# Key tokens in tiles of 128, z copies by way of DRAM, a new opening, one product moved from VectorE, and new program orders

## The chip, the cores and the metric

The kernel runs on one core of a Trainium2 chip. The metric is the device time of one execution in microseconds (us); a kernel is judged by the median of several runs. The engines are TensorE (PE; its weight loads are listed as PEld), VectorE (DVE), ScalarE (ACT), GpSimd (POOL) and SyncE (SP), which here only starts transfers (DMAs). Each engine works through its own program in order and waits on semaphores.

## The reference

The input x holds 32 images of 56 x 56 pixels with 32 channels, in f32. For each image, in short:

```python
x = x + conv3x3(sign(batchnorm(groupnorm(x))), sign(W) * scale)
t = tokens(x)                                   # 3136 tokens of 32 channels
n = layernorm(t)
q, k, v = elu(n@wq + b) + 1, elu(n@wk + b) + 1, n@wv + b         # 16 heads of 32
kv_cos, kv_sin = sum_s (k*cos)^T v, sum_s (k*sin)^T v            # linear attention
o = (q*cos)@kv_cos + (q*sin)@kv_sin
t = t + dense(o / (q*cos . sum k*cos + q*sin . sum k*sin + 1e-5))
n2 = layernorm(t)
w = the two largest of softmax(n2 @ router), scaled to sum 1
t = t + sum over those two of w_e * (n2 @ expert_e + b_e)        # 8 experts
```

The statistics of the batch norm go over all 32 images, so all of x is read once before any image can begin.

## The kernel before

**Tiling.** An image's 3136 tokens lie in 7 tiles. A tile holds 112 patches of 2 x 2 pixels, so there are 28 slots (7 tiles by 4 pixel positions g) of 112 tokens. In "patch layout" a matrix has 128 rows (4 positions by 32 channels) and 784 patches.

**Steps.** The work on an image is cut into named steps, and each engine does its share of a step. XT loads the image and turns it; CV is the convolution (SP copies the thresholded image `nat` to `shifted` first); XC centers it, SM1 and PN1 make the first layernorm `xn`. ZT turns `xn` back and splits it into a high and a low f16 half, `zhl`. SP then copies `zhl` into `z1`, 16 DMAs (lines 464 to 471), so that each of the four g has its high and low rows on 128 partitions. ZU does the same for the second layernorm, into `z2`. K computes keys: two matmuls of 512 columns (line 551), an exponential on ACT (688), a max/min on DVE into `kbuf` (975), two buffers. KX multiplies the keys with `xcs`, the tokens times cos and sin, which POOL makes in CS (797); its two matmuls are in f32 and write the two halves of one bank (560). KT and G turn the sum into the matrices for the queries. Q computes queries like K (576, 693, 981). DN, SU, RC, RL and RH make the reciprocal of the denominator. R and RP spread it over the heads with a matmul (602) and multiply the queries: channel half 0 of each of the 7 tiles on DVE, straight from the bank (R, line 996), half 1 by an ACT copy into `spread_r` (725) and a POOL product (802) (RP). NM and T2 form the attention output; S2, SM2 and PN2 the second layernorm; LG and RT the router; F the experts (DVE 1058, POOL 841 to 847); OUT the store.

**Order.** The order of the steps on each engine is written out by hand in the table `ORDER`: each step has a time in units of which 14 make one iteration, and each iteration of the walk runs the steps of up to seven images, shifted against each other. Most matmul results go to a ring of three pairs of banks (K, Q, R, RP, F, ...); a step takes a pair when the step three places before it in PE's order has been read. SP, too, is in order: it waits for what a transfer needs, starts it, and goes on to the next.

**Opening.** SP loads x in eight parts of four images into two buffers `stage`; PE turns them, DVE takes their statistics. Then come the weights and the tables. PE begins with the first image when ACT has folded `wv` and `wd` into `p2`, DVE has the thresholds and all tables are there.

Of the kernel before, what the change touches and what calls it, by code (L numbers as in the profile page):

```python
# [6 lines left out]
F32 = mybir.dt.float32  # L7
# [15 lines left out]
TOKENS = HW * HW  # L23
DH = HEADS * C
# [3 lines left out]
HALF = (4, 3)  # L28
COL = [(0, 4 * PT), (4 * PT, 7 * PT)]
# [9 lines left out]
def consts():  # L39
# [31 lines left out]
    tabk = cs.transpose(3, 0, 1, 2).reshape(PT, 2 * SLOTS)  # L71
# [21 lines left out]
class Img:  # L93
# [10 lines left out]
    def par(self):  # L104
# [29 lines left out]
    },  # L134
    "vector": {
# [16 lines left out]
    },  # L152
    "scalar": {
# [17 lines left out]
    },  # L171
    "gpsimd": {
        "RP": [20.36, 21.80, 23.22, 26.00, 26.75, 27.35, 28.06],
        "F": [42.89, 44.35, 45.46, 46.69, 47.39, 51.02, 52.51],
        "T2": [26.80, 29.79, 32.86, 34.18],
        "RL": [19.34, 24.68],
        "CS": [-1.95, 6.49],
        "PN2": [35.08],
        "PN1": [-4.03],
        "OUT": [54.08],  # L180
        "RF": [40.46, 40.76],
        "GT": [41.80],
    },
    "sync": {
        "OUT": [42.36],
        "ZT": [-9.43],
        "CV": [-23.34],
        "XT": [-35.15],
        "ZU": [24.07],
# [51 lines left out]
def build(nc, x, gamma, beta, conv_taps, conv_rows, wq, wk, wv, wd, wd_b, we, eyec, eyem, mean4, pair, dsum, sel,  # L241
          p2c, tabdc, tabnc, tabkc, firstc, validc, out):
    ctx = ExitStack()
    with ctx:
# [16 lines left out]
        tabk = sb("tabk", [PT, 2, SLOTS])  # L261
# [28 lines left out]
        xcs = sb("xcs", [PT, SLOTS, 2, C])  # L290
# [3 lines left out]
        kbuf = sb("kbuf", [PT, 2, 1024])  # L294
# [19 lines left out]
        stage = [qflat[0:PT, k * 3584:(k + 1) * 3584].rearrange("p (b f) -> p b f", b=4) for k in range(2)]  # L314
# [28 lines left out]
        weights_in = sem("weights_in")  # L343
        tables_in = sem("tables_in")
# [3 lines left out]
        stage_in = [sem(f"stage_in{k}") for k in range(2)]  # L348
# [23 lines left out]
        zlow_made = [sem(f"zlow_made{k}") for k in (1, 2)]  # L372
        z_in = [sem(f"z_in{k}") for k in (1, 2)]
# [36 lines left out]
        READ = {"K": (k_made, 14), "R": (qr_made, 7), "RP": (r_copied, 7), "Q": (q_made, 14), "G": (g_made, 2),  # L410
# [8 lines left out]
        def _(sp):  # L419
            sp.dma_start(eye_center[:, :], eyec).then_inc(eye_in, 16)  # L420
            x4 = x.rearrange("(q b) h w c -> q b (h w c)", b=4).rearrange("q b (p f) -> q p b f", p=PT)
            for k in range(2):
                sp.dma_start(stage[k], x4[k]).then_inc(stage_in[k], 16)
# [60 lines left out]
        def _(pe):  # L484
# [3 lines left out]
            for q in range(8):  # L488
                pe.wait_ge(stage_in[q % 2], 16 * (q // 2) + 16)
                for b in range(4):  # L490
                    if 4 * q + b >= 4:
                        pe.wait_ge(stage_read, 4 * q + b - 3)
                    for j in range(TILES):
                        dst = ps[:, 2 * b + (j >= 4), (j % 4) * PT:(j % 4 + 1) * PT]
                        mm = pe.transpose(dst, stage[q % 2][:, b, j * 128:(j + 1) * 128], eye[0:PT, 0:PT])
                    mm.then_inc(stage_turned, 1)
# [7 lines left out]
            pe.wait_ge(weights_in, 16 * 11)  # L504
            pe.wait_ge(dve_pre, 4)
            for h in range(HEADS):
                mm = pe.matmul(ps[:, 2, C * h:C * h + C], wvr[:, 128 * h:128 * h + 128], wd_s[:, C * h:C * h + C], start=True, stop=True)
            mm.then_inc(pe_pre, 1)

            def step(kind, m, n, rd):  # L510
# [34 lines left out]
                elif kind == "K":  # L545
                    pe.wait_ge(z_in[0], m.at(256, 256))
                    if n == 0:
                        pe.wait_ge(weights_made, 1)
                    for k in range(2):
                        s = 2 * n + k  # L550
                        mm = pe.matmul(o[0:PT, k, :], z1[:, m.par, s % G, s // G, :], wk16[:, :], start=True, stop=True)  # L551
                    mm.then_inc(ring_full, 1)
                elif kind == "KX":
                    pe.wait_ge(k_made, m.at(14, n + 1))
                    if n in (0, 7):
                        pe.wait_ge(xcs_made, m.at(2, n // 7 + 1))
                    if n == 0:
# [555 lines left out]
```

## Time and profile before

| | |
|---|---|
| median of 3 runs | 2426.46 us (2424.11 to 2431.5) |
| the profiled execution's own time | 2426.23 us |
| its span, from the first to the last instruction | 2424.4 us |
| busy, share of the span | PE 93%, DVE 85%, ACT 66%, POOL 76% |
| 16 DMA engines, share of the span | 21.3% |
| matmuls | 15908 |

Busy shares are means over an opening, a long middle part in which images follow each other, and an end. The rows that the prediction uses stand in a section of their own below.

### The profile page before, as it was taken

Reading aid. Unit: us, or ns where it says so; the run is one execution under the profiler, and the core shown is the slowest. Engines: PE = TensorE matmul, PEld = TensorE weight load, DVE = VectorE, ACT = ScalarE, POOL = GpSimd, SP = SyncE. Lnnn points to the kernel's source line nnn. Section 1 sums busy time; section 2 is a strip of 40 time slices with the busy share of each in tenths; the row PEclk is TensorE's granted clock in tenths of the full one; section 3 lists DMA queues with packets and bytes.
Section 4 is the critical chain, followed back from the end, with each engine's and each line's share of the span. In section 5 each row is a group of like instructions: output and inputs, shape, how many; then the busy total and the mean of one; then the engine's idle time right before and its main releaser. Section 6 shows DMA issues by size and latency. Waiting matters only on the chain.

```text
span 2424.4 us, 45391 instructions
## 1 busy us (share of the span) xinstructions
PE 2252.8 (93%) x15908; PEld 1126.0 (46%) x15908; DVE 2064.4 (85%) x2725; ACT 1589.9 (66%) x2789; POOL 1841.0 (76%) x1553
## 2 busy tenths in 40 slices
PE   4369999999999999999999999999999999999971
PEld 4324444444544444444544444454544444454441
DVE  5357899999999999999999999999999999998852
ACT  0157777777777777777777777777777777777620
POOL 0414588888888888888888888888888888888775
PEclk8589999999999999999999999999999999999985
DMA  7421112222221112222221212222211212211001
GB/s 209 112 39 22 32 29 44 35 42 45 45 44 34 36 34 43 34 44 44 45 42 36 34 37 40 35 45 45 45 39 37 37 36 40 36 38 35 21 21 27
DMA packets 284863, 105.31 MB, mean 43 GB/s; under 512 B 246032, under 2 KB 279680, under 8 KB 284512
## 3 DMA queue, kind: packets, MB, share of 16 engines
q1 hardware_dynamic: 284640, 102.41, 21.3%
q8 instruction: 131, 2.15, 0.4%
q14 instruction: 92, 0.75, 0.1%
HBM read 31.19 MB, written 12.85 MB: 18 GB/s over the span
## 4 chain that ended last, share of the span: by engine, by line
PE 67%; DVE 15%; ACT 6%; issue 5%; POOL 3%; DMA 2%; SPq 1%; POOLq 0%; DVEq 0%; ACTq 0%
PE ps L560 15%; PE ps L611 12%; PE ps L551 7%; PE ps L602 6%; PE ps L576 5%; PE ps L585 5%; DVE qbuf L981 4%; DVE prod L1058 4%; ACT ebuf L693 3%; DVE kbuf L975 3%; PE ps L542 2%; PE ps L535 2%; PE ps L630 2%; DVE den L993 2%; PE ps L530 2%
## 5 line engine op out<-in xcount | busy, mean ns | idle before, releaser
L975 DVE SCALAR_TENSOR_TENSOR kbuf<-ps,ebuf 112x1024 f32<-112x1024 f32 x448 | 546.2, 1219 | 114.3 <-ACT ebuf L688 111.8
L693 ACT ACTIVATE ebuf<-ps,small 128x896 f32<-128x896 f32 x448 | 450.3, 1005 | 195.0 <-PE ps L576 113.1
L688 ACT ACTIVATE ebuf<-ps,small 112x1024 f32<-112x1024 f32 x448 | 498.3, 1112 | 107.4 <-PE ps L551 87.8
L981 DVE SCALAR_TENSOR_TENSOR qbuf<-ps,ebuf 128x896 f32<-128x896 f32 x448 | 486.5, 1086 | 43.2 <-ACT ebuf L693 38.7
L802 POOL TENSOR_TENSOR qbuf<-spread_r,qbuf 128x896 f32<-128x896 f32 x224 | 469.0, 2094 | 21.4 <-ACT spread_r L725 21.4
L560 PE MATMUL ps<-kbuf,xcs 112*64 112x512 f32 x1792 | 474.9, 613 | 4.1 <-DVE kbuf L975 4.1
L785 POOL TENSOR_TENSOR rstd<-varr,power 112x28 f32<-112x28 f32 x64 | 307.2, 4800 | 137.7 <-DVE varr L960 137.5
L611 PE MATMUL ps<-qbuf,gmat 128*64 128x224 f32 x3584 | 390.1, 360 | 3.0 <-POOL qbuf L802 2.2
L611 PEld LDWEIGHTS ps<-qbuf,gmat 128*64 128x64 f32 x3584 | 243.7, 138 | 165.0 <-issue 77.8
L1058 DVE TENSOR_TENSOR prod<-ps,gate 112x1024 f32<-112x1024 f32 x224 | 271.2, 1212 | 29.6 <-POOL ffn L847 10.1
L551 PE MATMUL ps<-wk,z 128*112 128x512 f16 x896 | 280.1, 395 | 15.7 <-issue 12.6
L841 POOL TENSOR_TENSOR prod<-prod 112x512 f32<-112x512 f32 x224 | 285.5, 1275 | 1.5 <-DVE prod L1058 1.4
L725 ACT ACTIVATE spread_r<-ps 128x896 f32<-128x896 f32 x224 | 204.6, 913 | 82.2 <-PE ps L602 53.8
L576 PE MATMUL ps<-z,wq 128*128 128x448 f16 x896 | 245.5, 356 | 6.2 <-DVE qbuf L981 3.3
L602 PE MATMUL ps<-rs,sel 128*128 128x448 f16 x896 | 240.8, 357 | 10.5 <-ACT rs L719 4.3
L996 DVE TENSOR_TENSOR qbuf<-ps,qbuf 128x896 f32<-128x896 f32 x224 | 237.3, 1083 | 7.2 <-PE ps L602 4.6
L585 PE MATMUL ps<-qbuf,dmat 128*32 128x448 f32 x1792 | 231.9, 549 | 0.2
L551 PEld LDWEIGHTS ps<-wk,z 128*112 128x112 f16 x896 | 93.6, 129 | 206.7 <-DVE qbuf L981 74.0
L844 POOL TENSOR_TENSOR prod<-prod 112x256 f32<-112x256 f32 x224 | 163.4, 730 | 17.6
L560 PEld LDWEIGHTS ps<-kbuf,xcs 112*64 112x64 f32 x1792 | 101.7, 136 | 146.5 <-issue 116.1
L636 PE MATMUL ps<-we,z 128*112 128x256 f16 x896 | 145.0, 287 | 11.2 <-DVE prod L1058 10.4
L636 PEld LDWEIGHTS ps<-we,z 128*112 128x112 f16 x896 | 97.1, 133 | 83.3 <-issue 24.1
(131 smaller groups left out, 3052.6 us busy)
## 6 DMA issues: line engine op xcount, KB each, us to landing
z<-zhl SPq DMA_DIRECT2D x1024, 49.0 KB, 1.9
qbuf<-in_x SPq DMA_DIRECT2D x8, 1568.0 KB, 8.9
xt<-in_x SPq DMA_DIRECT2D x256, 49.0 KB
out<-ffn SPq DMA_DIRECT2D x256, 49.0 KB
shifted<-nat SPq DMA_DIRECT2D x128, 52.6 KB, 5.0
qbuf<-in_sel SPq DMA_DIRECT2D x1, 1024.0 KB, 13.2
tabn<-in_tabnc SPq DMA_DIRECT2D x1, 784.0 KB, 12.5
p<-in_p2c SPq DMA_DIRECT2D x1, 528.0 KB, 9.6
```

What stands on the lines that cost most here:

```text
L551: mm = pe.matmul(o[0:PT, k, :], z1[:, m.par, s % G, s // G, :], wk16[:, :], start=True, stop=True)
L560: mm = pe.matmul(kt_bank[64 * k:64 * k + 64, :], xcs[:, 2 * n + k, :, :].rearrange("p a c -> p (a c)"), kbuf[:, n % 2, DH * k:DH * k + DH] ...
L576: mm = pe.matmul(o[:, k, 0:G * PT].rearrange("p (g t) -> p g t", g=G), wq16[:, 128 * (k0 + k):128 * (k0 + k) + 128], z1[:, m.par, :, j, :] ...
L585: mm = pe.matmul(o[32 * j:32 * j + 32, 0:HW4], dmat[:, m.par, c, :, :].rearrange("p a h -> p (a h)"), qbuf[:, c, 4 * h + j, :], start=(c = ...
L602: mm = pe.matmul(o[:, k, 0:HW4], sel16[:, 128 * a:128 * a + 128], rs[:, j // 4, :], start=True, stop=True)
L611: mm = pe.matmul(o[64 * v:64 * v + 64, 0:2 * PT].rearrange("p (a t) -> p a t", a=2), gmat[:, m.par, c, :, :].rearrange("p a o -> p (a o)") ...
L688: act.activation(ebuf[0:PT, 0, :].rearrange("p (a b) -> p a b", a=2), o[0:PT, :, :], ACT.Exp, bias=minus_one[0:PT, :]).then_inc(kexp_made, 1)
L693: act.activation(ebuf[:, 1, 0:2 * G * PT].rearrange("p (a b) -> p a b", a=2), o[:, :, 0:G * PT], ACT.Exp, bias=minus_one).then_inc(qexp_ma ...
L802: nc.gpsimd.tensor_tensor(qbuf[:, 2:4, n, :], spread_r[:, :, :], qbuf[:, 2:4, n, :], ALU.mult)\
L975: v.scalar_tensor_tensor(kbuf[:, n % 2, :].rearrange("p (a b) -> p a b", a=2), o[0:PT, :, :], 1.0, ebuf[0:PT, 0, :].rearrange("p (a b) -> ...
L981: v.scalar_tensor_tensor(qbuf[:, k0:k0 + 2, j, :], o[:, :, 0:G * PT], 1.0, ebuf[:, 1, 0:2 * G * PT].rearrange("p (a b) -> p a b", a=2), AL ...
L1058: v.tensor_tensor(prod[:, n % 2, :, :].rearrange("p s (e c) -> p (s e) c", c=C), o[0:PT, :, :].rearrange("p k (s c) -> p (k s) c", c=C), g ...
```

## The change

- **Keys.** Keys are computed for 24 tiles of 128 tokens and one of 64 instead of 28 of 112: `KT` = 25 matmuls in `KS` = 13 steps, for K and for KX. The tokens for KX must lie in the same tiles: SP writes `xn` to a DRAM tensor `xd` (four DMAs, step CS0 of SP) and reads it back as `xkt` (two DMAs, CS1), and POOL makes `xcs` from `xkt`.
- **z.** The 16 copies become one store of `zhl` to DRAM (`zd`), a wait of SP for it, and four loads.
- **The queries' product.** For tile 1 both halves are done the RP way; R has 6 steps and RP 8.
- **Opening.** x goes through four buffers of two images; the first image's own load stands ahead of the weights; the weights are in two groups with a semaphore each; `wv` times `wd` goes to bank 7, and ACT's fold into `p2` and the waits for the tables move into the steps that first need them.
- **Program orders.** All five lists of `ORDER` are new.

```diff
+KT = -(-TOKENS // 128)
+KREST = TOKENS - 128 * (KT - 1)
+KS = (KT + 1) // 2
+KH = 6
+BOTH = (1,)
+R_TILES = [j for j in range(TILES) if j not in BOTH]
+RP_UNITS = [(j, h) for j in range(TILES) for h in ((1, 0) if j in BOTH else (1,))]
...
-            for k in range(2):
-                sp.dma_start(stage[k], x4[k]).then_inc(stage_in[k], 16)
+            for q in range(4):
+                sp.dma_start(stage[q], x2[q]).then_inc(stage_in[q], 16)
...
-            for q in range(2, 8):
-                sp.wait_ge(stage_turned, 4 * q - 4)
-                sp.dma_start(stage[q % 2], x4[q]).then_inc(stage_in[q % 2], 16)
+            for q in range(4, B // 2):
+                sp.wait_ge(stage_turned, 2 * q - 6)
+                sp.dma_start(stage[q % 4], x2[q]).then_inc(stage_in[q % 4], 16)
...
+            load(Img(None, 0))
...
                     sp.wait_ge(zlow_made[ln], m.at(2, 2))
+                    wait(sp, z_in[ln], m.at(64))
+                    sp.dma_start(zd[ln], zhl[ln][:, :, :]).then_inc(z_out[ln], 16)
+                    sp.wait_ge(z_out[ln], m.at(16, 16))
+                    src = zd[ln].rearrange("(g c) h f -> h c g f", g=G)
                     for r in range(4):
-                        for g in range(G):
-                            dst = z2[32 * r:32 * r + 32, g] if ln else z1[32 * r:32 * r + 32, m.par, g]
-                            sp.dma_start(dst.rearrange("p j t -> p (j t)"),
-                                         zhl[ln][32 * g:32 * g + 32, r % 2, :]).then_inc(z_in[ln], 16)
+                        dst = z2[32 * r:32 * r + 32] if ln else z1[32 * r:32 * r + 32, m.par]
+                        sp.dma_start(dst.rearrange("p g j t -> p g (j t)"), src[r % 2]).then_inc(z_in[ln], 16)
+                if kind == "CS" and n == 0:
+                    sp.wait_ge(xn_made[0], m.at(1, 1))
+                    wait(sp, xkt_in, m.at(32))
+                    for g in range(G):
+                        dst = xd[PATCHES * g:PATCHES * g + PATCHES].rearrange("(j t) c -> t j c", t=PT)
+                        src = xn[0][:, :, :].rearrange("p (j g) c -> p g j c", g=G)[:, g]
+                        sp.dma_start(dst, src).then_inc(xkt_out, 16)
+                if kind == "CS" and n == 1:
+                    sp.wait_ge(xkt_out, m.at(64, 64))
+                    wait(sp, xcs_made, m.at(2))
+                    sp.dma_start(xkt[:, 0:KT - 1, :], xd[0:128 * (KT - 1)].rearrange("(i p) c -> p i c", p=128)).then_inc(xkt_in, 16)
+                    sp.dma_start(xkt[0:KREST, KT - 1, :], xd[128 * (KT - 1):TOKENS]).then_inc(xkt_in, 16)
...
-                    for k in range(2):
-                        s = 2 * n + k
-                        mm = pe.matmul(o[0:PT, k, :], z1[:, m.par, s % G, s // G, :], wk16[:, :], start=True, stop=True)
+                    flat = z1[:, m.par, :, :, :].rearrange("p g j t -> p (g j t)")
+                    for k in range(2 if n < KS - 1 else 1):
+                        a, w = 128 * (2 * n + k), 128 if 2 * n + k < KT - 1 else KREST
+                        mm = pe.matmul(o[0:w, k, :], flat[:, a:a + w], wk16[:, :], start=True, stop=True)
...
-                    for k in range(2):
-                        mm = pe.matmul(kt_bank[64 * k:64 * k + 64, :],
-                                       xcs[:, 2 * n + k, :, :].rearrange("p a c -> p (a c)"),
-                                       kbuf[:, n % 2, DH * k:DH * k + DH], start=(n == 0), stop=(n == 13))
+                    for k in range(2 if n < KS - 1 else 1):
+                        i = 2 * n + k
+                        w = 128 if i < KT - 1 else KREST
+                        mm = pe.matmul(kt_bank[64 * k:64 * k + 64, :], xcs[0:w, i, :, :].rearrange("p a c -> p (a c)"),
+                                       kbuf[0:w, m.at(KS, n) % 2, DH * k:DH * k + DH], start=(n == 0), stop=(i >= KT - 2))
...
-            pe.wait_ge(act_pre, 1)
             pe.wait_ge(dve_pre, 6)
-            pe.wait_ge(tables_in, 16 * 9)
...
-                    nc.gpsimd.tensor_tensor(qbuf[:, 2:4, n, :], spread_r[:, :, :], qbuf[:, 2:4, n, :], ALU.mult)\
+                    j, half = RP_UNITS[n]
+                    q = qbuf[:, 2 * half:2 * half + 2, j, :]
+                    pool.wait_ge(r_copied, m.at(NP, n + 1))
+                    nc.gpsimd.tensor_tensor(q, spread_r[:, :, :], q, ALU.mult)\
```

In the new order one iteration of SP is: XT, ZU, CS0, CV, ZT, CS1, OUT (before: OUT, ZT, CV, XT, ZU). A stretch of PE's new order, from ZU to LG, is: ZU1, K10, XT0, KX8, RP3, Q1, XT1, KX9, K11, NM1, RP4, R1, KX10, R2, ZT0, Q2, NM2, R3, RP5, LG. From ZT to the next image's first KX it is: ZT1, T20, R4, Q4, Q5, NM3, RP7, Q6, KX12, NM4, G0, G1, NM5, R5, Q7, T21, F0, Q8, T22, F1, Q9, DN0, DN1, F2, Q10, DN2, K0, DN3, K1, Q11, SU0, K2, NM6, KX0; then F3, K3, KX1, RP0, KX2, T23, R0, F4, K4. (T20 to T23 are the four steps T2.)

## Rows read from the trace of the kernel before

**Rows 1.** Stretch, its us, busy (count) PE, PEld, DVE, ACT, POOL; clock, DMA, GB/s.
```profile
1000.00:1200.00 200.00, 199.35 (x1431) 98.54 (x1427) 183.62 (x240) 146.19 (x258) 166.40 (x139) 1.00 0.20 39
```

**Rows 2.** The chain that ended last, whole run: start us, us, what.
```profile
282.76 1.87 PE ps L560 x8
...
2194.53 1.87 PE ps L560 x8
```

**Rows 3.** The same chain, within one image's period.
```profile
1016.81 0.57 PE ps L551 x2
...
1028.10 0.86 PE ps L560 x4
...
1029.88 0.43 PE ps L551 x2
1030.31 1.01 PE ps L560 x4
...
1036.83 1.67 PE ps L611 x16
1038.49 0.53 PE ps L542 x4
...
1042.39 0.40 PE ps L602 x2
...
1044.45 0.48 PE ps L602 x2
```

**Rows 4.** Groups of instructions: shapes, count; busy us, mean ns; idle before.
```profile
L975 DVE SCALAR_TENSOR_TENSOR kbuf<-ps,ebuf 112x1024 f32<-112x1024 f32 x448 | 546.2, 1219 | 114.3 <-ACT ebuf L688 111.8 <-PE ps L560 0.3
...
L560 PE MATMUL ps<-kbuf,xcs 112*64 112x512 f32 x1792 | 474.9, 613 | 4.1 <-DVE kbuf L975 4.1
L802 POOL TENSOR_TENSOR qbuf<-spread_r,qbuf 128x896 f32<-128x896 f32 x224 | 469.0, 2094 | 21.4 <-ACT spread_r L725 21.4
...
L996 DVE TENSOR_TENSOR qbuf<-ps,qbuf 128x896 f32<-128x896 f32 x224 | 237.3, 1083 | 7.2 <-PE ps L602 4.6
...
L797 POOL TENSOR_TENSOR xcs<-xn,tabk 112x448 f32<-112x448 f32 x128 | 117.8, 942 | 0.2
```

**Rows 5.** Timeline from a ZU to the LG that needs its z: start, us.
```profile
1026.25 0.89 PE L542 MATMUL ps<-eye_center,xn 112*128 112x112 f32 x7
...
1028.54 10.29 SPq L470 DMA_DIRECT2D z<-zhl  x16
...
1040.82 1.36 PE L630 MATMUL ps<-we,z 128*112 128x8 f16 x24
```

**Rows 6.** DMA issues: count, KB each, median us from issue to landing.
```profile
z<-zhl SPq DMA_DIRECT2D x1024, 49.0 KB, 1.9
qbuf<-in_x SPq DMA_DIRECT2D x8, 1568.0 KB, 8.9
...
shifted<-nat SPq DMA_DIRECT2D x128, 52.6 KB, 5.0
```

**Rows 7.** The chain in the opening, 0 to 70 us.
```profile
27.41 8.67 DMA qbuf<-in_x
...
55.38 8.61 DMA qbuf<-in_x
...
64.04 4.20 PE ps L495 x21
```

**Rows 8.** Busy time by engine in a stretch of the opening.
```profile
30.00:40.00 10.00, 4.21 (x25) 4.00 (x24) 4.97 (x11) 0.00 (x0) 0.00 (x0) 0.73 1.03 273
```

**Rows 9.** Timeline of the opening, all engines.
```profile
82.91 1.28 ACT L654 ACT_TABLE_LOAD   x1 [82.91 <-PE ps L507]
...
84.56 0.15 DVE L927 COPY small<-small 128x1 f32<-128x1 f32 x1
...
86.64 1.01 PE L521 MATMUL ps<-eye_center,xt 112*128 112x112 f32 x4 [3.82 <-ACT p L654]
...
130.65 1.93 PE L551 MATMUL ps<-wk,z 128*112 128x512 f16 x4 [12.61 <-issue]
```

More of the change, by code:

```diff
@@ L152 @@
+        "SM1": [-11.08],
+        "ZU": [30.95, 31.39],
+        "XT": [-24.26, -24.17],
+        "RC": [11.46, 18.02],
+        "R": [12.96, 18.69, 18.77, 19.28, 20.57, 23.13],
+        "ZT": [-9.06, -7.96],
+        "LG": [33.34],
+        "RT": [34.58, 35.36, 35.96, 36.51, 36.71, 37.05],
     },
     "scalar": {
[17 rows of a table removed]
+        "ZU": [28.02, 28.71],
+        "K": [-4.42, -3.99, -2.45, -1.94, -1.52, -1.14, -0.84, -0.49, -0.21, 0.23, 0.78, 1.80, 4.55],
+        "SU": [9.97, 14.55],
+        "XT": [-27.01, -26.78],
@@ new lines @@
+        "RP": [12.12, 12.54, 13.65, 15.08, 16.64, 17.30, 18.72, 20.70],
+        "Q": [-0.36, 1.78, 3.10, 4.69, 5.31, 6.03, 6.94, 7.41, 8.09, 8.51, 9.01, 10.04, 12.89, 13.27],
+        "RC": [10.14, 16.27],
+        "RH": [11.87, 16.66],
+        "ZT": [-11.25, -8.84],
+        "LG": [32.59],
+        "T2": [19.24, 21.94, 22.17, 26.18],
+        "KT": [6.83],
+        "RT": [35.03],
+        "G": [7.18, 7.40],
+        "S2": [24.99, 25.88, 26.49, 27.04],
+        "TB": [12.37],
+        "XC": [-14.01],
@@ L171 @@
     },
     "gpsimd": {
[L173 to L182, printed above, removed]
+        "RP": [10.18, 13.67, 14.95, 16.87, 18.30, 19.00, 19.14, 20.76],
+        "F": [35.33, 35.65, 37.08, 37.38, 38.24, 43.15, 46.85],
@@ L183 @@
+        "PN1": [-12.27],
+        "RL": [9.31, 16.89],
+        "OUT": [47.05],
+        "RF": [33.10, 33.36],
+        "T2": [19.80, 20.90, 23.37, 24.21],
+        "GT": [34.66],
+        "CS": [-5.29, -4.67],
+        "PN2": [27.73],
     },
     "sync": {
[L185 to L189, printed above, removed]
+        "XT": [-41.69],
+        "ZU": [14.70],
+        "CS": [-24.14, -16.17],
+        "CV": [-36.65],
+        "ZT": [-19.15],
@@ L190 @@
+        "OUT": [39.95],
     },
@@ L313, in build @@
         qflat = qbuf[:, :, :, :].rearrange("p a b c -> p (a b c)")
-        stage = [qflat[0:PT, k * 3584:(k + 1) * 3584].rearrange("p (b f) -> p b f", b=4) for k in range(2)]
+        stage = [qflat[0:PT, k * 1792:(k + 1) * 1792].rearrange("p (b f) -> p b f", b=2) for k in range(4)]
         at, views = 2 * 3584, {}
@@ L343, in build @@
         weights_in = sem("weights_in")
+        folds_in = sem("folds_in")
         tables_in = sem("tables_in")
@@ L347, in build @@
         eye_in = sem("eye_in")
-        stage_in = [sem(f"stage_in{k}") for k in range(2)]
+        stage_in = [sem(f"stage_in{k}") for k in range(4)]
         stage_turned = sem("stage_turned")
@@ L372, in build @@
         zlow_made = [sem(f"zlow_made{k}") for k in (1, 2)]
+        zd = [nc.dram_tensor(f"zd{k}", [128, 2, PATCHES], F16).ap() for k in (1, 2)]
+        z_out = [sem(f"z_out{k}") for k in (1, 2)]
+        xd = nc.dram_tensor("xd", [TOKENS, C], F32).ap()
+        xkt_out = sem("xkt_out")
+        xkt_in = sem("xkt_in")
         z_in = [sem(f"z_in{k}") for k in (1, 2)]
@@ L487, in _ @@
             pe.wait_ge(eye_in, 16)
[L488 to L496, printed above, removed]
+            for img in range(B):
+                q, b = img // 2, img % 4
+                pe.wait_ge(stage_in[q % 4], 16 * (q // 4) + 16)
+                if img >= 4:
+                    pe.wait_ge(stage_read, img - 3)
+                for j in range(TILES):
+                    dst = ps[:, 2 * b + (j >= 4), (j % 4) * PT:(j % 4 + 1) * PT]
+                    mm = pe.transpose(dst, stage[q % 4][:, img % 2, j * 128:(j + 1) * 128], eye[0:PT, 0:PT])
+                mm.then_inc(stage_turned, 1)
             pe.wait_ge(consts_in, 16 * 5)
@@ L605, in step @@
                 elif kind == "NM":
-                    pe.wait_ge(qr_made, m.at(7, n + 1))
-                    pe.wait_ge(qp_made, m.at(7, n + 1))
+                    wait(pe, qr_made, m.at(NR, len([j for j in R_TILES if j <= n])))
+                    pe.wait_ge(qp_made, m.at(NP, len([j for j, _ in RP_UNITS if j <= n])))
                     for c in range(CH):
@@ L647, in _ @@
         def _(act):
-            act.wait_ge(tables_in, 16 * 9)
-            act.wait_ge(pe_pre, 3)
-            for v in range(2):
-                for cs in range(2):
-                    q = slice(64 * v + 32 * cs, 64 * v + 32 * cs + 32)
-                    dst = p2[q, :, cs, :, 0:C]
-                    last = act.activation(dst, ps[q, 2, :].rearrange("p (a h o) -> p a h o", a=CH, h=HPC), ACT.Copy,
-                                          scale=SHIFT)
-            last.then_inc(act_pre, 1)
             act.wait_ge(dve_pre, 6)
@@ L680, in step @@
                     ln = kind == "ZU"
+                    if m.c == 0 and n == 0 and kind == "ZT":
+                        act.wait_ge(tables_in, 16 * 9)
+                        act.wait_ge(pe_pre, 3)
+                        for v in range(2):
+                            for cs in range(2):
+                                q = slice(64 * v + 32 * cs, 64 * v + 32 * cs + 32)
+                                last = act.activation(p2[q, :, cs, :, 0:C],
+                                                      ps[q, 7, :].rearrange("p (a h o) -> p a h o", a=CH, h=HPC), ACT.Copy,
+                                                      scale=SHIFT)
+                        last.then_inc(act_pre, 1)
                     act.wait_ge(ring_full, no + 1)
-                    wait(act, z_in[ln], m.at(256))
+                    wait(act, z_out[ln], m.at(16))
                     a, b = COL[n]
@@ L713, in step @@
                     act.wait_ge(recip_made, m.at(2, n + 1))
-                    wait(act, qr_made, m.at(7, -3 if n == 0 else 0))
+                    wait(act, qr_made, m.at(NR, -len([j for j in R_TILES if j >= 4]) if n == 0 else 0))
                     act.activation(r_high[:, :], den[:, 0:HALFW], ACT.Copy).then_inc(rhigh_made, 1)
@@ L788, in step @@
                     wait(pool, high_made[ln], m.at(2))
+                    if not ln:
+                        wait(pool, xkt_out, m.at(64))
                     nc.gpsimd.tensor_tensor(xn[ln][:, :, 0:C - 1], xc[ln][:, :, 0:C - 1],
@@ L867, in _ @@
             v.memset(nat[:, :, :], 1.0)
+            v.memset(xkt[:, KT - 1:KT, :], 0.0)
             v.memset(dmat[:, :, :, :, :], 0.0)
@@ L984, in step @@
                 elif kind == "DN" and n % 4 == 3:
+                    if m.c == 0 and n == 3:
+                        dve.wait_ge(tables_in, 16 * 9)
                     h = n // 4
```

105 lines of the change are left out of this document (61 added, 44 removed), and 67 rows, old and new, of the table ORDER.

## The prediction, made before the change was run

> **What bounds the kernel now.** I first read a stretch in the middle of the run by engine [rows 1]. The reader is to see that TensorE (PE) is busy 199.35 of 200 us at the full granted clock, VectorE (DVE) 183.62, GpSimd (POOL) 166.40 and ScalarE (ACT) 146.19, with DMA at 0.20. Next I read the chain of the whole run [rows 2]: the same double KX step comes back at 282.76 and at 2194.53 us, 28 images later, so an image costs 68.28 us and 31 images after the first cost 2117 of the 2424.4 us. Then I read one period of that chain [rows 3]. Its pieces are PE steps laid end to end; a K step (two matmuls) takes 0.43 or 0.57 us, a KX step 0.86 or 1.01. So PE's list of steps is the period, and an edit is worth what it takes off that list, as long as no other engine or transfer then holds PE up. The opening (first K of the first image at 130.65 us, [rows 9]) and the end, where one image runs alone, are chains of waits of their own.
>
> **Fewer K and KX steps.** Before, an image has 28 slots of 112 tokens: 14 K steps and 14 KX steps. After, it has 25 tiles of 128 (the last of 64): 13 steps each, the last of one matmul. From [rows 3]:
> - KX: one step less, 0.86 to 1.01 us; I take 0.95. The four records of a step last 0.61 us each on average [rows 4] but a step is over in 0.86, so its two matmuls, which write different halves of the bank, run beside each other. The single matmul of the last step therefore saves nothing more.
> - K: one step less, 0.43 to 0.57; I take 0.50. The last step has one matmul instead of two: half of 0.43, 0.21.
> Together 1.66 us an image (1.50 to 1.79). DVE loses two K passes of 1.22 us and gets one half as wide (about 0.69, by the width), 1.75 us less; ACT loses in the same proportion.
>
> **One product moved.** Tile 1's first half leaves DVE (1.08 us) and goes to ACT (one more copy) and POOL (2.09) [rows 4]. PE's matmuls for it stay. DVE now needs 62.7 - 1.75 - 1.08 = 59.9 us an image (183.62/200 of 68.28, less these), 90% of a 66.6 us period where it had 92%. POOL needs 56.8 + 2.09, and its CS passes shrink from 3.77 to 25/28 of that, so 58.5 us, 88% of the period where it had 83%. Both still end inside the period, so I cost the move at nothing; it is PE's list that hides it. If that cover went, it would cost POOL's 2.09 less DVE's 1.08, about 1 us an image.
>
> **New program orders.** The order of PE's steps changes everywhere, and a step's cost depends on its neighbour by some 0.15 us [rows 3]; kinds follow each other about as often as before, so I take no difference. DVE is locally the denser engine between F0 and the next image's K4, where five F and five K passes (K's takes 1.22 us, [rows 4]) stand close together. Three ring slots lie between PE and DVE, so I bound what PE waits there by nothing and one such pass, 1.22 us, and take 0.15, since DVE's share falls. Per image: -1.66 + 0.15, about -1.5; over 31 images **-46.5 us** (-55 to -9).
>
> **z by way of DRAM.** The 16 copies of z (16 issues in 10.29 us, then 1.9 us to land [rows 5, 6]) become one store to DRAM, a wait on SP for it, and four loads. No row of before shows a store to DRAM that is waited for. From below I take the 1.9 us of the small copy; from above I add the size: a load of 1568 KB lands in 8.9 us [rows 6], 0.0046 us a KB more, so 392 KB would take 3.5 us, and the last loads, 784 KB in all, 1.9 to 3.4 us after the last issue. From the last ZU matmul to the first copy is 1.4 us before (1027.14 to 1028.54, [rows 5]). After: 1.4 + 0.64 + 1.9 (3.5) + 4 x 0.64 + 1.9 (3.4) + 0.1 = 8.5 to 11.6 us; I take 10.5, nearer the upper end because that one counts the bytes. What is behind this is LG, which needs z of the second layernorm. In the new PE order there lie between ZU1 and LG two K, three KX, six R or RP, two Q, two NM, two XT and one ZT step. With Q priced like K, R at 0.40 to 0.48 and the last three at no more than 0.53 each, that is 1.0 + 2.9 + 2.6 + 0.9 + 3.3 + 1.3 = 12.0 us [rows 3]. So LG just does not wait; before, it was the same race (12.3 us from first issue to LG, [rows 5]). The Trainium skill (DMA: Bandwidth & Descriptors, Anatomy of one DMA) speaks against this edit: it puts about 2.0 us of fixed cost on each DMA, most of it the receipt of the write and heaviest where the target is HBM, and here it is paid twice in a row; no row here shows such a receipt. By its fit (2.0 us plus the bytes at 436 GB/s, for another way of issuing) I estimate the path at 10.1 us, and the sum would be the same.
>
> SP stands still while it waits for that store. Behind it in SP's order are CS1 (the reload of the keys' tokens), OUT and the next XT load; the latter two are due most of a period later. The first layernorm's z is followed by K0, and the keys' tokens go out (four DMAs of 784 pieces of 128 bytes) and come back (3072 pieces): 1.4 + 0.64 + 3.5 + 2.6 + two issues 1.3 + 5.0 (what a shift of 928 pieces of 58 bytes takes, [rows 6]) + two CS passes 1.9 = 16.3 us from ZT1 to KX0. Between those stand four NM, one KX, eight Q, three R or RP and three K steps, 6.7 + 1.0 + 3.6 + 1.3 + 1.5 = 14.1 us, and thirteen steps of other kinds not counted in it. So it fits, at no cost.
>
> **The opening.** Before, PE waits three times for x, 8.67 us the first time and 8.61 the last [rows 7], since a part's load starts only when its buffer was read. The 8 loads of 1568 KB are 12.8 MB; at the 273 GB/s of the stretch from 30 to 40 us [rows 8] they need 47 us, and PE's 224 transposes, at 4.20 us for 21, 44.8 us. With four buffers of half the size both overlap: the transposes end at best near 51 us instead of 68.2 (-17), at worst one wait goes (-8); I take -13. PE no longer waits for ACT's work on p2 (start 86.64 against 84.71 when DVE is done, [rows 9]: -1.9), but the table load (1.28) moves behind the first threshold: -0.6. On the other side, SP now issues four stores of xn and the second image's four shifts before z of the first image: eight issues of 0.64 us, partly under the ZT steps, so some 3 us later, and z and then xkt queue behind their small pieces; KX0 needs xkt, which it did not before. I put that at +4.5 (0 to +10). Together **-9 us** (-19 to +2). **The end**: one ZU path of 12.3 us becomes about 10.5, **-2** (0 to -4).
>
> **The sum**, on the profiled execution: 2424.4 - 46.5 - 9 - 2 = 2366.9 us of span, and 1.8 us lie around the span (its time is 2426.23): 2368.7. The median of the three runs, 2426.46, is 0.2 above that execution, so 2369.
>
> **Rivals.**
> - *DVE or POOL becomes the bound* in part of the period (DVE between F0 and K4, or POOL, whose 58.5 us also hold waits for the routing and for spread_r). For it: both are at 90% and 88%, and they run lists in fixed order. Against it: DVE's load falls. A period of 67.4 to 68.0 us gives 2392 to 2416.
> - *LG waits for z*, the rival on the other side. The price is 31 us for each us by which the path outlasts 12.0 us. It takes back the whole gain (57.5 us) when it is late by 1.9 us, that is with a path of 13.9 us; at 14.5 us the kernel takes 2446. For it: a stored and waited-for DRAM write is unknown here, and the margin is 0 to 3 us. Against it: even the size-counting end is 11.6 us, and the queue is not loaded (DMA 0.20). The Trainium skill's rule on the write's receipt (same page, same section) is this mechanism.
> - *The change is hidden*: the period shrinks by half a us and the opening by nothing, 2419 to 2434. PE's list would have to be no bound, against [rows 1].
> - *Better ends on all terms*: 2424.4 - 55 - 19 - 4 + 1.8 = 2348 and a little below.
>
> **How the numbers follow.** Forecast as summed, 2348 to 2392: 0.55. DVE or POOL: 0.19. LG late: 0.12. Hidden: 0.06. Better: 0.08. A measurement of this kernel tells about 0.3% (7 us) from no change. Faster is 0.55 + 0.19 + 0.08 = 0.82, same 0.06, slower 0.12. The predicted time is 2369 us. The range 2342 to 2414 takes in the forecast, nearly all of the second case and most of the better one, about 8 in 10.
>
> **What would show it.** In the profile after: the same KX step recurring every 66.5 to 67 us; 13 KX and 13 K steps an image; PE still above 99% busy in the middle; DVE near 90%, POOL near 88%; no recurring wait of LG for z or of POOL's CS for xkt; the last bn_stats near 55 us; the first K near 122 to 127 us. I am wrong if PE is well below 99% in the middle, with LG or a K step waiting for a DMA, or with the ring waiting for DVE, or if the period is right and the opening is not shorter.

## The result and the profile after

The changed kernel takes 2417.58 us (median of 11 runs, 2402.14 to 2421.86) where the kernel before takes 2427.9 in the same comparison (2424.11 to 2433.57): a ratio of 0.9947, 95% interval 0.993 to 0.9964. The forecast was 2369 us, in a range of 2342 to 2414, so the prediction was wrong: faster, but by 10 us and not by 57. The profiled execution took 2408.88 us, with a span of 2407.1; it is the second shortest of the 11, so the median execution is some 9 us longer than the one that the rows below show.

In the middle of the run, by engine (columns as in [rows 1]):

```profile
1000.00:1200.00 200.00, 195.94 (x1432) 95.56 (x1430) 179.01 (x233) 145.84 (x260) 171.96 (x142) 1.00 0.35 65
...
1800.00:2000.00 200.00, 194.20 (x1418) 94.26 (x1414) 179.35 (x231) 143.56 (x259) 174.76 (x147) 1.00 0.35 61
```

Against [rows 1] TensorE has lost its 99%: 3.4 to 5.2 us more idle time in 200, and VectorE and ScalarE are no busier. Only GpSimd and the DMA engines work more. No engine is full, so something that is no engine's work sets the pace.

How long an image takes is read from an instruction that occurs once in it. I take POOL's step OUT (line 878, in which `ffn` and `t` are added), here in POOL's timeline for the first image and for the 28th (after that one the images run out and the gaps shrink):

```profile
352.61 2.09 POOL L878 TENSOR_TENSOR ffn<-ffn,t 112x896 f32<-112x896 f32 x1
...
2200.50 2.08 POOL L878 TENSOR_TENSOR ffn<-ffn,t 112x896 f32<-112x896 f32 x1
```

27 gaps in 1847.89 us are 68.44 us each. The same instruction in the kernel before:

```profile
360.72 2.09 POOL L835 TENSOR_TENSOR ffn<-ffn,t 112x896 f32<-112x896 f32 x1
...
2204.91 2.09 POOL L835 TENSOR_TENSOR ffn<-ffn,t 112x896 f32<-112x896 f32 x1
```

These are gaps of 68.30, as the recurring step of [rows 2] says. **The steady part gained nothing**; it lost 3.7 us. The 17.3 us between the two spans come from the ends, which gained 21.0: the first OUT is 8.1 us earlier, and from the 28th OUT to the last instruction it takes 206.6 us, not 219.5.

What sets the 68.44 shows in the chain that ended last, here from one image's OUT to the next image's first F on POOL:

```profile
1589.35 1.99 POOL ffn L878
...
1591.36 0.52 DVE zhl L1014
...
1591.90 2.35 DMA zd<-zhl
...
1594.27 0.31 SPq L493
...
1596.10 0.38 SPq L504
...
1596.52 3.40 SPq L505
...
1604.83 1.71 DMA out<-ffn
...
1606.67 1.28 POOL prod L884
```

SP holds the output for 8.6 us after it is ready. POOL's OUT is over at 1591.4, but SP has just begun on z: the store of `zhl` (2.35 us until it has landed), four loads (1.73 in all), two loads of key tokens, of which the second and small one (64 tokens) takes 3.40 us to issue. Only at 1599.96 does it reach the eight stores of the output (5.28 us), and the last of them lands at 1606.54. POOL waits for that landing, because F of the next image writes the one buffer `ffn` (line 883, a wait on `out_stored`). POOL's timeline around it, the bracket being the idle time and its releaser:

```profile
1604.28 0.63 POOL L850 TENSOR_TENSOR xc<-t,mean 112x256 f32<-112x256 f32 x1
1606.67 1.27 POOL L884 TENSOR_TENSOR prod<-prod 112x512 f32<-112x512 f32 x1 [1.76 <-DMA out<-ffn]
```

The page's groups give the whole run's idle time in that place (last columns), and the sizes of the other edited steps:

```profile
L884 POOL TENSOR_TENSOR prod<-prod 112x512 f32<-112x512 f32 x224 | 285.6, 1275 | 79.9 <-DMA out<-ffn 55.7
...
L597 PE MATMUL ps<-kbuf,xcs 128*64 128x512 f32 (+1 forms) x1600 | 449.4, 619 | 3.2 <-POOL xcs L838 1.8
...
L1043 DVE TENSOR_TENSOR qbuf<-ps,qbuf 128x896 f32<-128x896 f32 x192 | 208.6, 1086 | 11.6 <-PE ps L641 9.4
```

The reader is to see 55.7 us of waiting for `out<-ffn`, most of what the image period is above the 66.2 us that turn out below (27 times 2.2, or 60). The edits themselves came out as planned: 1600 KX records in place of 1792 at the same length as in [rows 4], 192 passes of R on VectorE in place of 224.

DMA issues of the new paths (count, KB each, median us from issue to landing):

```profile
z<-zd SPq DMA_DIRECT2D x256, 196.0 KB, 3.7
zd<-zhl SPq DMA_DIRECT2D x64, 392.0 KB, 2.4
...
xkt<-xd SPq DMA_DIRECT2D x32, 384.0 KB, 6.3
```

The opening, in PE's and POOL's timelines: last transposes of x, the first image's XT, its first K, its first CS.

```profile
60.69 2.88 PE L529 MATMUL ps<-eye_center,qbuf 112*128 112x112 f32 x14 [0.50 <-DMA qbuf<-in_x]
77.33 1.01 PE L555 MATMUL ps<-eye_center,xt 112*128 112x112 f32 x4
...
124.65 2.72 PE L586 MATMUL ps<-wk,z 128*128 128x512 f16 x6 [14.58 <-issue]
...
127.38 3.31 POOL L838 TENSOR_TENSOR xcs<-xkt,tabk 128x384 f32<-128x384 f32 x4 [18.93 <-DMA xkt<-xd]
```

In PE's timeline of the kernel before, the last transposes of x are these:

```profile
64.04 5.18 PE L495 MATMUL ps<-eye_center,qbuf 112*128 112x112 f32 x28 [5.73 <-DMA qbuf<-in_x]
```

Transposes end at 63.57 (69.22 before; the chain of [rows 7] leaves TensorE after 21 of these 28, at 68.24), XT starts at 77.33 and K at 124.65 (86.64 and 130.65, [rows 9]).

### The profile page after: what moved, and what is told of

Read it like the earlier page. It is cut to its first block, busy times and chain, and to the rows that moved or that the text cites. A ratio compares the mean times of both kernels' runs of the same rounds, so it can differ in the third digit from the quotient of the medians.

```text
span 2407.1 us, 44360 instructions
## 1 busy us (share of the span) xinstructions
PE 2201.8 (91%) x15620; PEld 1085.5 (45%) x15620; DVE 2001.0 (83%) x2662; ACT 1566.6 (65%) x2789; POOL 1898.4 (79%) x1585
## 4 chain that ended last, share of the span: by engine, by line
POOL 38%; PE 25%; SPq 10%; issue 8%; DVE 7%; DMA 7%; ACT 4%; POOLq 0%; DVEq 0%; ACTq 0%
POOL qbuf L845 11%; POOL rstd L824 8%; POOL prod L884 6%; PE ps L597 5%; PE ps L650 4%; SPq L511 4%; SPq L505 4%; POOL prod L887 4%; POOL xn L830 3%; DMA zd<-zhl 3%; PE ps L614 2%; PE ps L641 2%; PE ps L586 2%; PE ps L623 2%; DVE kbuf L1019 2%
## 5 line engine op out<-in xcount | busy, mean ns | idle before, releaser
L845 POOL TENSOR_TENSOR qbuf<-spread_r,qbuf 128x896 f32<-128x896 f32 x256 | 536.1, 2094 | 31.9 <-ACT spread_r L764 28.6
L1019 DVE SCALAR_TENSOR_TENSOR kbuf<-ps,ebuf 128x1024 f32<-128x1024 f32 (+1 forms) x416 | 488.3, 1174 | 83.1 <-ACT ebuf L727 72.2
L727 ACT ACTIVATE ebuf<-ps,small 128x1024 f32<-128x1024 f32 (+1 forms) x416 | 449.3, 1080 | 138.5 <-PE ps L586 83.5
L597 PE MATMUL ps<-kbuf,xcs 128*64 128x512 f32 (+1 forms) x1600 | 449.4, 619 | 3.2 <-POOL xcs L838 1.8
L884 POOL TENSOR_TENSOR prod<-prod 112x512 f32<-112x512 f32 x224 | 285.6, 1275 | 79.9 <-DMA out<-ffn 55.7
L764 ACT ACTIVATE spread_r<-ps 128x896 f32<-128x896 f32 x256 | 234.3, 915 | 114.3 <-PE ps L641 67.5
L586 PE MATMUL ps<-wk,z 128*128 128x512 f16 (+1 forms) x800 | 249.4, 391 | 63.3 <-DVE prod L1105 33.3
L1043 DVE TENSOR_TENSOR qbuf<-ps,qbuf 128x896 f32<-128x896 f32 x192 | 208.6, 1086 | 11.6 <-PE ps L641 9.4
L641 PEld LDWEIGHTS ps<-rs,sel 128*128 128x128 f16 x896 | 61.9, 100 | 209.2 <-issue 87.9
L586 PEld LDWEIGHTS ps<-wk,z 128*128 128x128 f16 (+1 forms) x800 | 61.0, 98 | 200.9 <-DVE prod L1105 66.9
L597 PEld LDWEIGHTS ps<-kbuf,xcs 128*64 128x64 f32 (+1 forms) x1600 | 85.3, 135 | 142.3 <-issue 126.4
## 6 DMA issues: line engine op xcount, KB each, us to landing
qbuf<-in_x SPq DMA_DIRECT2D x16, 784.0 KB, 10.3
```

The lines of the kernel that those rows point to most:

```text
L586: mm = pe.matmul(o[0:w, k, :], flat[:, a:a + w], wk16[:, :], start=True, stop=True)
L597: mm = pe.matmul(kt_bank[64 * k:64 * k + 64, :], xcs[0:w, i, :, :].rearrange("p a c -> p (a c)"), kbuf[0:w, m.at(KS, n) % 2, DH * k:DH * k ...
L641: mm = pe.matmul(o[:, k, 0:HW4], sel16[:, 128 * a:128 * a + 128], rs[:, j // 4, :], start=True, stop=True)
L727: act.activation(ebuf[0:w, 0, 0:DH * c].rearrange("p (a b) -> p a b", a=c), o[0:w, 0:c, :], ACT.Exp, bias=minus_one[0:w, :]).then_inc(kexp ...
L845: nc.gpsimd.tensor_tensor(q, spread_r[:, :, :], q, ALU.mult)\
L884: nc.gpsimd.tensor_tensor(p[:, :, 0:4 * C], p[:, :, 0:4 * C], p[:, :, 4 * C:], ALU.add)\
```

## The experiments

Three theories went into the first four. **A**: a closed loop, in which SP holds the store of the output behind z and the key tokens, POOL's F waits for it, and the delay comes back through the period to the same place. **B**: POOL has too much work since the product moved. **C**: TensorE or VectorE waits for z or key tokens from DRAM.

**1. The store of the output ahead of z on SP.**

```diff
-        "OUT": [39.95],
+        "OUT": [36.80],
```

> Edit: in SP's program order the store of an image (OUT) stands ahead of ZT's store and loads and of CS1, instead of last; nothing else differs from the changed kernel. Theory A (a closed loop: POOL's F0 waits until the previous image's output is stored, the store is issued by SP only after ZT and CS1, ZT waits for ACT, ACT for POOL's products): the loop is cut, the period falls from 67.9 us to between 66.4 and 67.2 us (it may be held a little by the key tokens, which now come about 5 us later), 2370 to 2395 us, ratio to the kernel before 0.976 to 0.986. Theory B (POOL simply has too much work, 175 of 200 us): period stays 67.9, ratio 0.995. Theory C (PE or DVE waits for z or the key tokens from DRAM): later ZT makes it slower, ratio above 1.0.

Measured: 2344.99 us, ratio 0.9665 (0.9651 to 0.968). POOL's OUT of the first and 28th image, and the middle by engine:

```profile
351.57 2.08 POOL L878 TENSOR_TENSOR ffn<-ffn,t 112x896 f32<-112x896 f32 x1
...
2139.11 2.10 POOL L878 TENSOR_TENSOR ffn<-ffn,t 112x896 f32<-112x896 f32 x1
```

```profile
1400.00:1600.00 200.00, 198.40 (x1455) 97.23 (x1456) 184.58 (x239) 147.60 (x263) 177.68 (x149) 1.00 0.34 67
```

27 gaps of 66.21 us. SP's timeline shows why:

```profile
1611.31 3.57 SPq L511 DMA_DIRECT2D out<-ffn  x8
1614.98 0.35 SPq L488 DMA_DIRECT2D zd<-zhl  x1
```

POOL's OUT ends at 1611.28 and the store is issued in the same moment; F0 starts at 1624.76, 13.5 us after OUT. In the changed kernel POOL is at F0 equally 13.5 us after OUT (1606.67 less 1.76, against 1591.4), but the store lands after 15.1. With the store first, POOL no longer waits for it (its row has 21.6 of its 21.7 us of idle time from VectorE), z leaves 3.2 us after its data is ready, and in the middle of the run nothing waits for it. TensorE is busy again for 198.4 of 200 us, and the chain's share of PE goes from 25% to 80%. A stands, but the gain is larger than the 0.976 to 0.986 that it foretold. B had foretold no change and C a slower kernel.

**2. Two `ffn` buffers, SP's order as in the changed kernel.** F then waits for the store of two images earlier. To make room, `mean4` lies in `xres` and `den` has 320 columns.

```diff
-        ffn = sb("ffn", [PT, SLOTS, C])
+        ffn = sb("ffn", [PT, 2, SLOTS, C])
...
-                        wait(pool, out_stored, m.at(128))
+                        wait(pool, out_stored[m.par], 128 * (m.c // 2))
```

> Edit: the experts' output ffn has two buffers, each with its own store semaphore, so that POOL's F0 waits only for the store of two images before; SP's order is that of the changed kernel (mean4 lies in xres and den is cut to 320 columns to make room). Theory A (loop through SP's OUT and POOL's F0): the loop is cut without making anything later, period 66.3 to 66.8 us, 2366 to 2385 us, ratio to the kernel before 0.974 to 0.983. Theory B (too much POOL work): no change, ratio 0.995. Theory C (waits for z or the key tokens): no change, ratio 0.995.

Measured: 2346.5 us, 0.967 (0.9654 to 0.9686); gaps of 66.21 us. The store is as late as ever (in SP's timeline its last issue ends at 1625.98, 13.8 us after POOL's OUT at 1612.15), but F0 starts at 1625.64 without it: only what waits for it has been taken away. So it is this wait, and not the place of z, the load on the queue or the work on POOL. (Here too the ratio lies below A's range, 0.974 to 0.983.)

**3. The product back on VectorE, SP's order as in the changed kernel.**

```diff
-BOTH = (1,)
+BOTH = ()
```

with R's seventh step put back (at 16.28 on TensorE, 16.29 on VectorE) and RP's unit taken out.

> Edit: the product that was moved goes back from ACT and POOL to DVE (R has 7 steps, RP 7, the steps at the places where they stood on PE). Theory A (loop): POOL's share of the loop is 2.09 us and one wait shorter, so the period falls to what PE's list allows, 66.3 to 66.8 us, ratio 0.974 to 0.983. Theory B (too much POOL work): the same, 0.974 to 0.983. Theory C (waits for z or the key tokens): no change, 0.995.

Measured: 2421.55 us, 0.998 (0.9966 to 0.9995); gaps of 69.25 us. All three theories missed, C's "no change" (0.995) by the least. POOL has 2.09 us less to do and waits longer:

```profile
L884 POOL TENSOR_TENSOR prod<-prod 112x512 f32<-112x512 f32 x224 | 285.3, 1274 | 99.5 <-DMA out<-ffn 60.0
```

B falls, as it did in experiments 1 and 2, where POOL's work is the same and the time is gone; C fell there as well. A survives with a correction: the long part of the loop, from F0 to the next OUT and z, can't be POOL's list alone. My reading, which no run tests by itself, is that all engines' lists run from F0 on and are delayed with it, so that when one of them gets shorter, another (here VectorE's, 1.08 us longer) stands in its place.

**4. z by the 16 copies of before, all else as in the changed kernel.**

```diff
-                    sp.dma_start(zd[ln], zhl[ln][:, :, :]).then_inc(z_out[ln], 16)
-                    sp.wait_ge(z_out[ln], m.at(16, 16))
...
+                        for g in range(G):
+                            sp.dma_start(dst.rearrange("p j t -> p (j t)"),
+                                         zhl[ln][32 * g:32 * g + 32, r % 2, :]).then_inc(z_in[ln], 16)
```

> Edit: z is copied by 16 DMAs inside SBUF again, without the store to DRAM and SP's wait for it; all else is the changed kernel. Theory A (loop): the 16 issues take about 10 us of SP where store, wait and four loads took 4.2, so the loop grows by 5 to 6 us: period 73 to 74 us, about 2590 us, ratio 1.05 to 1.07. Theory B (too much POOL work): no change, 0.995. Theory C (the DRAM detour of z costs the time): faster than the changed kernel, period 66.3 to 67, ratio 0.975 to 0.985.

Measured: 2630.72 us, 1.0854 (1.0813 to 1.0896). The path by DRAM, with its wait, is shorter on SP than 16 issues, so C has the wrong sign here; A has the right one, but its range (1.05 to 1.07) was too low. POOL's row:

```profile
L882 POOL TENSOR_TENSOR prod<-prod 112x512 f32<-112x512 f32 x224 | 284.9, 1272 | 200.9 <-DMA out<-ffn 172.5
```

The second four ask what the parts are worth once the loop is open.

**5. Experiments 1 and 3 together** (store first, product back).

> The store of the output ahead of z in SP's order, as in the first experiment, and the moved product back on VectorE (R 7 steps, RP 7). Theory A: the loop over SP is open, so TensorE's list of 66.2 us sets the period whether the product is on VectorE or not; VectorE goes from 61.0 to 62.1 us of it. Then 2345 us (2340 to 2352), 0.965 to 0.969 of before, no difference to the first experiment that can be told. Rival D: VectorE at 94% of the period holds TensorE up in its dense part by 0.3 us an image or more, so that the move is worth something now: 2354 to 2375, 0.970 to 0.978.

Measured: 2358.26 us, 0.9709 (0.9697 to 0.9722); gaps of 66.66 us.

```profile
1400.00:1600.00 200.00, 197.72 (x1441) 96.00 (x1442) 185.18 (x241) 143.73 (x259) 170.64 (x145) 1.00 0.34 65
```

Rival D: the moved product is worth 0.45 us an image in the profiled executions, and 0.0044 of the time before by the two ratios, some 11 us, with some 5 either way. In the table of PE's waits for the middle of the run (us in total, times, longest), one appears that experiment 1 does not have, for VectorE's step R:

```profile
PE ps L569 <- DVE qbuf L1043: 6.3, 27, 0.4
```

The step put back has one place in the order, which I chose; another might cost less.

**6. Experiments 1 and 4 together** (store first, z by 16 copies).

> The store of the output first in SP's order, and z by the 16 copies of before in place of the store to DRAM and four loads. Theory A: the 16 copies cost 4 us more of SP's time for each z, but SP's own list then stays under 45 us of a period of 66.2, and what is behind z has TensorE steps of 12 us or more to cover the 12.3 us of the path; so 2345 to 2375 us, 0.966 to 0.978. Rival C (z's path decides, and its way by DRAM is what the change won): more than 2400 us, 0.99 or above.

Measured: 2451.0 us, 1.0092 (1.0074 to 1.0109); gaps of 69.42 us. A's numbers failed here and C's held. LG does wait, in PE's timeline (the first row is the last step of ZU):

```profile
1591.32 0.51 PE L574 MATMUL ps<-eye_center,xn 112*128 112x112 f32 x3
...
1605.24 1.58 PE L667 MATMUL ps<-we,z 128*112 128x8 f16 x28 [1.57 <-DMA z<-zhl]
...
1607.98 1.98 PE L595 MATMUL ps<-kbuf,xcs 128*64 128x512 f32 x4
```

LG is not all: in the last row a KX step takes 1.98 us and not 1.08, and the granted clock (third column from the end) of the stretches around it shows why:

```profile
1595.00:1603.00 8.00, 8.00 (x56) 3.65 (x53) 7.63 (x9) 6.06 (x10) 7.83 (x6) 1.00 0.31 77
...
1607.10:1612.20 5.10, 5.10 (x26) 2.38 (x26) 2.78 (x6) 3.13 (x6) 2.82 (x3) 0.68 1.02 73
1612.20:1620.00 7.80, 7.80 (x86) 4.28 (x86) 7.32 (x15) 5.40 (x13) 2.84 (x3) 1.00 0.44 98
```

After the wait and LG, TensorE runs part of 5.1 us at 1.2 GHz instead of 2.4: at 0.68 that is 1.63 us of work lost. This is one image. For all 27 gaps, experiment 6 and then experiment 1:

```profile
354.22:2228.48 1874.26, 1822.19 (x12954) 882.64 (x12953) 1648.46 (x2132) 1317.08 (x2348) 1588.00 (x1325) 0.97 0.29 50
...
351.57:2139.11 1787.54, 1772.73 (x12955) 865.84 (x12953) 1648.00 (x2132) 1316.15 (x2348) 1587.26 (x1324) 1.00 0.35 65
```

An image is 3.21 us longer than in experiment 1: TensorE is idle 1.38 us more (LG's waits for z are 1.31 of it) and busy 1.83 us more with the same matmuls, at a mean granted clock of 0.97 instead of 1.00. The way by DRAM is thus a condition of the new order, which leaves z some 12 us.

**7. Experiment 1 with x loaded as before**, eight parts of four images through two buffers.

```diff
-            for q in range(4):
+            for q in range(2):
...
-            for q in range(4, B // 2):
-                sp.wait_ge(stage_turned, 2 * q - 6)
-                sp.dma_start(stage[q % 4], x2[q]).then_inc(stage_in[q % 4], 16)
+            for q in range(2, B // 4):
+                sp.wait_ge(stage_turned, 4 * q - 4)
+                sp.dma_start(stage[q % 2], x2[q]).then_inc(stage_in[q % 2], 16)
```

> The store of the output first in SP's order, and x again in eight loads of four images through two buffers. Only the opening differs from the first experiment. If the last transposes, 4.7 us later in the trace of before than in that of after, delay all that follows: 2350 us, 0.968 to 0.970. If another chain (z of the first image behind SP's other transfers) sets the first key step: 2345 us, 0.966 to 0.967.

Measured: 2354.88 us, 0.9692 (0.968 to 0.9705); gaps of 66.21 us. PE's timeline, last transposes and XT:

```profile
65.61 4.97 PE L529 MATMUL ps<-eye_center,qbuf 112*128 112x112 f32 x28 [5.21 <-DMA qbuf<-in_x]
86.27 1.01 PE L555 MATMUL ps<-eye_center,xt 112*128 112x112 f32 x4 [1.94 <-DVE small L971]
```

The last transposes end at 70.58, 8.0 us later than in experiment 1 (62.58), and XT, which also waits 1.94 us for VectorE, starts 9.9 us later (76.34 there). The profiled span is 11.3 longer; by the ratios it is 0.0027, 6.6 us, with some 5 either way. The first expectation fits better than the second; the delay passes through to the end.

**8. The store between z and the key tokens on SP**: OUT at 38.00.

> The changed kernel with the store of the output between z and the reload of the key tokens in SP's order (one place earlier, not two). Theory A: the loop loses the reload's two issues, 0.4 + 3.4 us, and the wait ahead of them, so 67.9 becomes 63 to 64 us, below TensorE's 66.2: 2345 to 2352 us, 0.966 to 0.970, as with the store ahead of z. If instead z and the wait for its store are what does the harm, wherever the reload stands: 2390 to 2420 us, 0.985 to 0.997.

Measured: 2346.38 us, 0.9653 (0.9639 to 0.9667); gaps of 66.21 us. SP's timeline:

```profile
1548.08 0.34 SPq L488 DMA_DIRECT2D zd<-zhl  x1
1550.44 1.73 SPq L493 DMA_DIRECT2D z<-zd  x4
1552.22 3.82 SPq L511 DMA_DIRECT2D out<-ffn  x8
```

The issues end at 1556.04, and POOL's F0, at 1561.04, finds the store done. The output may well stand behind z and its wait; behind the key tokens as well it comes too late.

The chain of cause in one table, from POOL's timeline and the page of each kernel (us; the wait is that of F for `out<-ffn` in the whole run). Rows in pairs differ in the place of OUT alone:

| kernel | gap, mean of 27 | gap with OUT first | 27 x the difference | F's wait |
|---|---|---|---|---|
| changed kernel | 68.44 | 66.21 (exp. 1) | 60 | 55.7 |
| product back (exp. 3) | 69.25 | 66.66 (exp. 5) | 70 | 60.0 |
| z by 16 copies (exp. 4) | 76.32 | 69.42 (exp. 6) | 186 | 172.5 |

In each pair F's wait, which the kernels with OUT first do not have at all, comes to 86 to 93% of the loss. The rest is not traced row by row; the mean granted clock of the 27 gaps is lower too where OUT is last (0.99, 0.98 and 0.93, against 1.00, 1.00 and 0.97).

## Why the prediction was wrong

**The step that failed** is the sentence on what stands behind SP's wait: "Behind it in SP's order are CS1 (the reload of the keys' tokens), OUT and the next XT load; the latter two are due most of a period later." For XT that holds. OUT is due 13.5 us after it is ready, when POOL begins the next image's F in the same buffer. In place of "no cost" the runs showed 55.7 us of waiting of F for `out<-ffn`; without that wait, cut in three ways (experiments 1, 2 and 8), an image takes 66.21 us and not 68.44, and the kernel 2345 to 2346.5 us. The stand-still was seen, and the order too; what was not asked was who waits for `out_stored`. The kernel before has the same wait (line 839), but there the store is done long before F, so no row shows it. The trace of before shows the slack that was spent, in SP's and POOL's timelines:

```profile
1043.71 2.08 POOL L835 TENSOR_TENSOR ffn<-ffn,t 112x896 f32<-112x896 f32 x1
...
1061.85 1.27 POOL L841 TENSOR_TENSOR prod<-prod 112x512 f32<-112x512 f32 x1
```

```profile
1045.82 3.59 SPq L477 DMA_DIRECT2D out<-ffn  x8
1049.45 10.52 SPq L470 DMA_DIRECT2D z<-zhl  x16
```

There OUT is first on SP and is issued as POOL ends it (1045.79); F0 comes 16.1 us after that. From these rows and the terms on record it could be worked out: with z, ready when OUT is, and the reload ahead, 0.64 + 1.9 to 3.5 + 4 x 0.64 + two issues 1.3 + 3.6 for the eight stores + 1.9 to land make 11.9 to 13.5 us, against the 16.1. POOL's new order has two RP products between OUT and F0 where the old one has three, which takes 2.09 us [rows 4] off the 16.1: a margin of 0.5 to 2.1 us, at 27 us of time for each us beyond it. It should have been a rival with a large chance; it was none. What ate the margin no row of before shows: the 64-token load and the stores behind it take 3.4 and 5.3 us to issue. The four rivals on record were others. "DVE or POOL becomes the bound" named an engine that does wait, POOL, but experiments 1 and 2 refute its mechanism: with the work of both engines unchanged the period is 66.21 us. Its time was also summed wrongly: a period of 67.4 to 68.0 us gives 2388 to 2407 by the prediction's own terms, not 2392 to 2416, and half a us an image in "the change is hidden" gives some 2411, not 2419 to 2434. That 2417.6 lies close to both means nothing.

The Trainium skill (DMA: Bandwidth & Descriptors, Anatomy of one DMA) says that a wait on a semaphore is made by the issuing sequencer, not by the DMA engines. The trace agrees: between the store at 1591.90 and the first load at 1594.27 SP issues nothing at all, though the output has been ready since 1591.4.

**Point by point**, with the loop open (experiment 1, where these terms can be seen):
- *Per image.* Forecast -1.66 from the steps, +0.15 for VectorE, so -1.5. Measured -2.09 (68.30 to 66.21), of which -1.64 remain with the product back (experiment 5). That agrees with the steps, but the new orders are in it too, and no run parts the two.
- *The moved product* was costed at nothing, and VectorE's easing at nothing too. It gains 0.45 us an image: with the step back on VectorE, TensorE waits for it (6.3 us in 27 images, above). VectorE's work was put at 59.9 us an image; experiment 1 has 61.0 (1648.00 in 27), 92% of its period, and was not free.
- *z by DRAM.* The store lands in 2.4 us (forecast 1.9 to 3.5), and LG does not wait in the middle of experiment 1. The 12.0 us of margin were right as well: in experiment 6 TensorE's steps fill 11.8 us from the end of ZU1 (1591.83) to the start of LG's wait (1603.67). The price of lateness, 31 us for each us, was too low: there it was 3.21 us an image for 1.31 of waiting, because TensorE also ran slower. (By the fit in the Trainium skill, same page and section, which is for another way of issuing, I estimate 2.9 us for 392 KB; the trace has 2.4.)
- *Key tokens.* They land in time in the middle; only in the opening does CS wait for them (18.93 us, above, and 19.14 for the second image).
- *The opening.* Forecast -9, measured -8.1 at the first OUT; that they are close is luck, since the terms are others. The transposes gained 5.6 us, not 13. The 8.67 and 8.61 us of [rows 7] are a load's whole time; TensorE's wait before the last part was 5.73 (row above), so a wait was worth less than the 8 of the forecast's lower bound. And from 0 to 60 us the DMA engines are busy 0.93 of the time at 225 GB/s, not at the 273 of [rows 8], which is one good stretch. Up to XT another 3.7 were won, against 1.9 in the forecast: XT no longer waits for ACT's `p2` (3.82 us, [rows 9]), and VectorE, whose end the forecast took for the next bound, was done earlier too (three of its last operations took 0.64 us in all, but 2.89 before and in experiment 7; why, no run shows). The table load behind the first threshold then took back 1.2 (forecast 1.28), and z's way to the first K 2.0 (14.58 us for 12.61; forecast 4.5 for z and `xkt`).
- *The end.* Forecast -2, and four images' share of the -1.5, so -8; measured -12.9, and -15.8 in experiment 1. LG waits for z there 20.6 us before and 10.3 in experiment 1: three waits and two, not one.

Had the store kept its place, 2345 us would still have been 24 below the forecast, inside its range.

## What to carry to other kernels

A wait on an engine that starts transfers is a wait for everything behind it in that engine's order. For each transfer behind it, ask when it becomes ready, who waits for its completion (a reader, and also whoever writes its source next) and how long after; the smallest of these is the room for the wait, and a store from a single buffer is the first to look at. When every engine idles and none is the bound, look for a loop over images: its sign here was one wait that came back in nearly every image. Cutting it (the store in an earlier place, a second buffer) gave the same time each way, 2345 to 2346.5 us; taking work off one engine in it (experiment 3) gave nothing.

## What the runs showed of the hardware

- In these runs the time to issue a transfer changed with what stood ahead of it. The reload's 64-token load (8 KB) takes 3.40 us on SP directly behind the 3072-piece load, and 2.03 us in experiment 8, where the output's stores went before both; eight stores of the output take 3.57 us in experiment 1 and 5.28 behind the reload.
- A wait of TensorE can cost more than its length. In experiment 6, 27 of LG's 32 waits for z were followed, within 3 us of LG's start, by a fall of the granted clock to 0.50 (1.2 GHz); over the 27 gaps the slower matmuls cost 1.83 us an image and the idle time 1.38. The length alone does not decide: two waits, and the clock (third column from the end) of the 6 us from the start of LG.

```profile
351.87 1.58 PE L667 MATMUL ps<-we,z 128*112 128x8 f16 x28 [0.71 <-DMA z<-zhl]
...
698.62 1.58 PE L667 MATMUL ps<-we,z 128*112 128x8 f16 x28 [1.43 <-DMA z<-zhl]
```

```profile
351.87:357.87 6.00, 6.00 (x44) 3.41 (x45) 2.90 (x6) 2.92 (x6) 5.03 (x4) 0.72 1.06 95
698.62:704.62 6.00, 6.00 (x57) 4.07 (x58) 3.50 (x7) 3.53 (x7) 5.42 (x4) 1.00 0.92 93
```
